# Graph attention kernel: POOL instead of DVE adds the edges' bias and makes the shared node's one-hot

## The reference, cut to what matters

```
logits  = einsum('ehd,ehd->eh', q[rows] * scale, k[cols]) + att_bias     # 8 heads of 64
row_max = segment_max(logits, rows)
p       = exp(logits - row_max[rows])
denom   = segment_sum(p, rows)
y       = segment_sum((p / denom[rows])[:, :, None] * v[cols], rows)
out     = y.reshape(n, 512) @ Wo + bo
```

## Time and profile before

| | |
|---|---|
| time, median of 3 runs | 3393.04 us (3389.54 to 3396.01) |
| the profiled execution's own time | 3388.5 us, its span 3386.7 us |
| busy over the whole span | PE 88%, DVE 85%, ACT 65%, POOL 65% |
| busy in the edge loop, 2000 to 2800 us | PE 94%, DVE 99.5%, ACT 98.4%, POOL 78% |
| the chain that ended last, by engine | POOL 26%, DVE 25%, issue 20%, PE 14%, DMA 8%, ACT 3% |

### The profile page before, as it was taken

One profiled execution on the slowest core, in us unless ns is written; L12 is line 12 of the kernel. 1 busy time (PEld: TensorE's weight loads), 2 busy tenths in 40 slices (PEclk: granted clock), 3 DMA queues, 4 the chain that ended last, 5 costly groups with the idle time before them and its releaser, 6 DMA issues.

```text
span 3386.7 us, 50546 instructions
## 1 busy us (share of the span) xinstructions
PE 2965.5 (88%) x11485; PEld 1732.4 (51%) x11610; DVE 2891.4 (85%) x8827; ACT 2207.6 (65%) x7734; POOL 2206.9 (65%) x2509
## 2 busy tenths in 40 slices
PE   6898888888887369999999999999999999889998
PEld 4554544544554135555555555555555555445554
DVE  9897777777776379999999999999999999867776
ACT  6332222222221059999999999999999999934443
POOL 0377777777777557777777777777777777511110
PEclk9898888888898689999999999999999999999999
DMA  6343333333332688878888887888888888411121
GB/s 205 81 135 102 106 107 100 102 101 107 104 104 67 224 287 256 253 253 254 256 257 254 257 259 252 258 258 253 257 256 252 257 256 259 145 66 69 68 70 55
DMA packets 258890, 615.16 MB, mean 182 GB/s; under 512 B 69451, under 2 KB 80023, under 8 KB 258338
## 3 DMA queue, kind: packets, MB, share of 16 engines
q0 software_dynamic: 144832, 443.72, 41.5%
q1 hardware_dynamic: 107414, 155.39, 15.1%
q10 hardware_dynamic: 6348, 12.80, 1.1%
HBM read 550.28 MB, written 61.49 MB: 181 GB/s over the span
## 4 chain that ended last, share of the span: by engine, by line
POOL 26%; DVE 25%; issue 20%; PE 14%; DMA 8%; ACT 3%; DVEq 2%; another core or an unknown queue 1%; ACTq 0%; SPq 0%; POOLq 0%
POOL rec_scratch L617 22%; DMA big<-kv_scratch,small 8%; DVE big L1374 6%; PE banks L1920 5%; DVE small L1272 5%; DVE big L1266 5%; PE banks L1949 4%; POOL big L638 3%; ACT big L799 3%; POOL small L645 2%; DVE big L992 2%; PE banks L1963 1%; PE banks L1874 1%; PE banks L1823 1%
## 5 line engine op out<-in xcount | busy, mean ns | idle before, releaser
L799 ACT ACTIVATE big<-big,small 128x65 f32<-128x65 f32 x6656 | 1625.9, 339 | 4.8
L638 POOL DMA_INDIRECT big<-kv_scratch,small x832 | 842.8, 1013 | 405.6 <-DVE small L1272 285.7
L617 POOL DMA_INDIRECT rec_scratch<-big,small x782 | 770.0, 985 | 340.4 <-issue 237.9
L1874 PE MATMUL banks<-big,small 128*128 128x260 f32 x3328 | 898.4, 393 | 96.1 <-POOL small L645 42.7
L1823 PE MATMUL banks<-big,small 128*128 x1664 | 876.5, 609 | 30.7 <-DMA big<-q_scratch 12.0
L1874 PEld LDWEIGHTS banks<-big,small 128*128 128x128 f32 x3328 | 597.4, 190 | 534.4 <-ACT big L799 243.0
L1374 DVE SCALAR_TENSOR_TENSOR big<-big,loS,banks 128x520 f32 x832 | 611.4, 735 | 20.2 <-PE banks L1874 18.6
L1731 PE MATMUL banks<-big 128*128 128x512 f32 (+1 forms) x1176 | 609.5, 666 | 19.5 <-DVE big L982 19.5
L1266 DVE TENSOR_TENSOR big<-banks,big 128x512 f32<-128x512 f32 x832 | 558.6, 671 | 43.9 <-PE banks L1823 25.7
L645 POOL TENSOR_SCALAR small<-iotaF,small 128x128 f32<-128x128 f32 x832 | 524.3, 630 | 54.1 <-PE banks L1874 28.2
L1272 DVE TENSOR_REDUCE small<-big 128x8 f32<-128x512 f32 x832 | 548.4, 664 | 0.0
(11 more groups left out here) (257 smaller groups left out, 2742.1 us busy)
## 6 DMA issues: line engine op xcount, KB each, us to landing
rowR<-lo_rows SPq DMA_DIRECT2D x97, 256.0 KB
big<-src_rows SPq DMA_DIRECT2D x97, 256.0 KB, 3.6
big<-in_x_dram SPq DMA_DIRECT2D x96, 256.0 KB, 2.8
big<-kv_scratch,small POOLq DMA_INDIRECT x832, 5.2
rec_scratch<-big,small POOLq DMA_INDIRECT x782
kv_scratch<-big SPq DMA_DIRECT2D x48, 260.0 KB
q_scratch<-big SPq DMA_DIRECT2D x48, 256.0 KB
kv_scratch<-big SPq DMA_DIRECT2D x48, 256.0 KB
```

Of the source, the lines that this page charges most:

```text
L617: e.indirect_dma_start(recd, bass.IndirectOffsetOnAxis(ap=ridx[:, c % 4, j:j + 1], axis=0), rec[:, 8 * c + j, :], None).then_inc(s_sc[c % ...
L638: e.indirect_dma_start(KV[:, vat(t):vat(t) + YW + D], None, KVd, bass.IndirectOffsetOnAxis(ap=recB[b_ % 4][:, t % 16, 9:10].bitcast(i32), ...
L799: ins = e.activation(heads(Vr(t), h, h + 1), heads(Vr(t), h, h + 1), ACT.Copy, scale=ph[:, h:h + 1])
L1874: ins = e.matmul(YB[t % 2][:, i, :], oh[t % 4], Vr(t)[:, 260 * i:260 * i + 260], start=True, stop=True)
```

## The change

Two instructions a block leave DVE's list and enter POOL's. `lb`, the addition of the bias, goes from DVE's step 0 (behind the last `rd`) to POOL's step 4 of the same block, in front of that step's gather. `Aoh` goes from DVE's step 6 to POOL's step 14, behind that step's gather and in front of its `one_hot`, as `last_node`; it has a semaphore of its own, `s_aoh`, for which `scale1` on PE waits. `s_bd` now rises once a block instead of twice.

```diff
+            def lb(b_):
+
+                q.wait_ge(s_rd, 16 * b_ + 16)
+                e.tensor_tensor(Lr[b_ % 2], Lr[b_ % 2], recB[b_ % 4][:, :, 0:8], ALU.add).then_inc(s_lb, 1)
+
             def one_hot(t):
...
+            def last_node(b_):
+
+                q.wait_ge(s_s1, b_)
+                e.tensor_scalar(Aoh[0:8, :], iotaF[0:8, :], llb[0:8, max(b_ - 1, 0):max(b_ - 1, 0) + 1], None, ALU.is_equal).then_inc(s_aoh, 1)
 
             for s in range(T + DEL + 2):
...
+                if s % 16 == 4 and 0 < s // 16 <= NB:
+                    lb(s // 16 - 1)
                 if s < T:
                     gather(s)
...
+                if s == 24:
+                    last_node(0)
+                if 24 < s < T and s % 16 == 14:
+                    last_node(s // 16)
                 if s - DEL - 2 >= 0:
                     one_hot(s - DEL - 2)
...
-                q.wait_ge(s_bd, 2 * b_)
+                q.wait_ge(s_bd, b_)
...
-            def lb(b_):
-
-                q.wait_ge(s_rd, 16 * b_ + 16)
-                e.tensor_tensor(Lr[b_ % 2], Lr[b_ % 2], recB[b_ % 4][:, :, 0:8], ALU.add).then_inc(s_lb, 1)
...
-                e.tensor_scalar(Aoh[0:8, :], iotaF[0:8, :], llb[0:8, max(b_ - 1, 0):max(b_ - 1, 0) + 1], None, ALU.is_equal).then_inc(s_bd, 1)
...
-                if at == 0:
-                    lb(b_)
...
-                q.wait_ge(s_bd, 2 * b_ + 2)
+                q.wait_ge(s_bd, b_ + 1)
+                q.wait_ge(s_aoh, b_ + 1)
```

More of the change, by code:

```diff
@@ L306, in build @@
         s_kv = sems("s_kv", 8)
-        s_oh, s_q1, s_pr, s_rd, s_lb, s_x2 = sem("s_oh"), sem("s_q1"), sem("s_pr"), sem("s_rd"), sem("s_lb"), sem("s_x2")
+        s_oh, s_q1, s_pr, s_rd, s_lb, s_x2, s_aoh = sem("s_oh"), sem("s_q1"), sem("s_pr"), sem("s_rd"), sem("s_lb"), sem("s_x2"), sem("s_aoh")
         s_f1, s_d1, s_zm, s_zs, s_za, s_cf = sem("s_f1"), sem("s_d1"), sem("s_zm"), sem("s_zs"), sem("s_za"), sem("s_cf")
```

## The result

The changed kernel takes 3393.99 us (median of 22 runs, 3389.41 to 3400.08), the kernel before, run beside it, 3389.49 us (median of 22, 3382.68 to 3398.11). The ratio is 1.0015, with a 95% interval of 1.0008 to 1.0021: some 5 us slower, where 10 us faster was forecast. The profiled execution has a span of 3395.4 us (before 3386.7), both at a mean granted clock of 0.941.

The account below looks back on a forecast made before the run. DVE was taken to set the pace, ACT close behind. `fwd1` 0.22 us later less 0.41 for `Aoh` gave -0.19 us a block, times 51 blocks 10 us: 3383 us from a median of 3393.04, range 3374 to 3407.

Parts of the forecast that it names:

- What bounds the kernel: Edge loop: DVE sets the pace, ACT has hardly anything in hand; the change is worth tenths of a us times 51 blocks.
- Together 0.61 us a block: DVE's list: 0.20 us back from `lb` and 0.41 from `Aoh`, 31 us over 51 blocks if nothing else changed.
- POOL, step 14: Shared node's one-hot on POOL: 0.63 us plus 0.02 between instructions, 0.65 us, arriving as 0.16 us in step 0.
- the gate: POOL, step 0's gather: 0.49 us of its 2.34 is a wait that a late POOL doesn't pay, leaving 1.84.
- Rival 2: Step 0's gather: the 0.49 us is paid anyway, `fwd1` 0.71 us late, +15 us, 3408; chance 0.18.
- POOL, step 4: The bias's addition on POOL, behind step 3's one-hot, was taken to last 0.41 us.
- rival 1: POOL's addition is dear, 0.64 us (+2 us) or 0.54 by the skill's rule (3390); 3388 to 3395; chance 0.26.
- The chain: Block's end, POOL's addition to PE's transpose to DVE's `fwd1`: DVE waits 0.42 us, `fwd1` comes 0.22 us later than before.
- From `fwd1` round to the next block's gate nothing else changes but `Aoh`: Rest of the block: only `Aoh`'s 0.41 comes off, so 0.22 - 0.41 = -0.19 us a block, 10 us.
- Late gathers: Step 15's gather often lands too late, hidden in DVE's wait before `fwd1`: nothing in the sum, up to 3 us in the range.
- ACT's cap: ACT idles 0.24 us a block, capping any DVE saving at 12 us, or 21 us with the disturbed blocks.

Follow-up runs that it names:

- e2: Changed kernel with the bias's addition back on DVE, so only the shared node's one-hot is on POOL; 3383.71 us, ratio 0.9985 to the kernel before.
- e7: Changed kernel with the shared node's one-hot in POOL's step 13 instead of 14; ratio 1.0024 to the kernel before.
- e1: Kernel before with only the bias's addition moved to POOL, `Aoh` left on DVE; 3397.0 us, ratio 1.0025.
- e11: e4 with `Bd` behind the product of step 6 instead of in front of it; ratio 0.9984 to the kernel before.
- e4: Changed kernel with `fwd1`'s output and the spread's constant in PSUM instead of SBUF; 3383.87 us, ratio 0.9983 to the kernel before.
- e9: Kernel before with 13 short dummy memsets on POOL in front of step 4's gather, nothing moved; ratio 1.0024.
- e5: Kernel before with eight short dummy memsets on POOL in front of step 4's gather, nothing moved; ratio 1.0015.

## Why the prediction was wrong, point by point

1. **What bounds the kernel, and what the change is worth at most: right.** DVE sets the pace, tenths of a us times 51 blocks: the blocks of 3 to 49 differ by 0.102 us, which by 51 is 5.2 us, and the medians by 4.5.
2. **"Together 0.61 us a block": right as DVE's entries** (0.212 + 0.385 = 0.597), **wrong as a gain.** The step that failed is "`Aoh` starts at 2270.84 and `Bd` at 2271.26: 0.42 us ... I take 0.41. `Bd` stays". `Aoh` took 0.27 us when no gather was near and 0.73 when one was the earlier trace rows; I read this as the price of `Aoh`. Half of it was the price of the gather: in blocks 3 to 49 of the kernel before, `Aoh` took 0.41 us to the next start in the 40 in which it began 0.32 us behind a gather's start, and 0.20 in the 6 with another distance. With `Aoh` gone, `Bd` stands at 0.32 us behind the same gather and pays +0.188. The move is worth 0.197, not 0.41 (one trace of e2: the same 0.197, and `lb` loses 0.056 of it).
3. **POOL, step 14: price right** (0.61 measured, 0.63 taken), **and the gate right.** The gather of step 15 comes 2.40 us behind that of step 14 and that of step 0 follows 1.85 us later (1.84 was forecast; 2.34 before). Rival 2 is out, and e7 shows it again. Counted from `fwd1`, the gather of step 0 starts at -8.03 us (median) both in the changed kernel and in e1, which has no one-hot in step 14, and the stall at `fwd1` is 0.161 against 0.154: the gate took up all of the 0.65, where I let 0.16 arrive.
4. **POOL, step 4: right.** The addition takes 0.44 us (0.41 taken), rival 1's 0.64 and 0.54 are out. The Trainium skill (GPSIMD Engine Reference, Engine selection) says about twice VectorE's time; against the 0.27 us of `lb` on DVE it was 1.6 times here.
5. **The chain: too long by a quarter of a us.** "`fwd1` comes 0.22 us later than before": measured from DVE's own steps it came 0.05 us earlier (0.161 of stall for 0.212 of `lb`). Of the 0.27 between, 0.16 is the delay that didn't arrive, 0.04 the chain from the start of the addition to `fwd1` (0.86 us at the median, 0.90 taken), and 0.06 that the addition starts 0.04 us ahead of the one-hot's recorded end rather than 0.02 behind it. This error was against the change. With it set right and nothing else, I would have forecast a still larger gain.
6. **"From `fwd1` round to the next block's gate nothing else changes but `Aoh`": the step that decides, and false.** `back1` +0.114 and the spread +0.145 are 0.26 us a block, 13 us, and with `Bd` 0.45 us, 23 us. The prediction has no term for this: it puts it at nothing. I had looked at POOL for when it is busy, when its gathers land and who waits for its results, not for what its instructions do to DVE's beside them, though the earlier trace rows show the same instruction at 0.27 and 0.73.
7. **Late gathers: larger than I allowed, and elsewhere.** The row that holds them grew by 0.10 us a block (51 x 0.10 = 5 us); I had put up to 3 us in the range, nothing in the sum, and said that they hide in the stall of `fwd1`. They stand in front of other `pr`s. On one trace each the size is uncertain: 10 waits for a gather behind `ya` in 46 blocks, before 4.
8. **ACT's cap: too tight.** I took 0.24 us of slack, 33.28 us a block at best. The median block of e11 takes 33.13, at the same work on ACT. In the changed kernel the cap never mattered: ACT waits 18.5 us over 41 waits, before 17.4 over 41.

```profile
ACT small L777 <- remote: 18.5, 41, 1.6
```

9. **Range and rivals.** 3394 lies in the range, by a mechanism that none of the rivals had. The errors had both signs: to the forecast of -0.19 us a block come +0.45 for the three hits, -0.27 for the chain and +0.10 for the gathers, which makes +0.09, where +0.10 was measured. And the 3383 was counted from the median of three runs, 3393.04, which lies 3.6 us above that of 22.

The rival that was missing reads: POOL's instructions, moved by some tenths of a us, lie down on DVE's two-input instructions. Its price could have been had from the earlier trace rows, 0.2 us for each instruction hit, and its place from the one-hot of step 4 and the gather of step 5 beside `back1` and the spread. Three such hits would have been an estimated 0.6 us a block, as much as the change takes off DVE; they were 0.45.

## What to carry to other kernels

Before you move work to POOL, list DVE's instructions that read two operands from SBUF and see which POOL instructions each of them lies beside now, and which it will lie beside after the shift: here the hits cost 0.45 us a block against the 0.60 that was taken off DVE. Two operands are not the only sign: `Aoh` has one tensor as input, in SBUF, with a column of SBUF as its scalar, and it was hit as well (0.41 for 0.20). An instruction whose duration has two values is telling of its neighbour, not of itself; if you take it away, the neighbour's price goes to the next in line. A hit instruction can be freed by one operand in PSUM or by a place behind one that doesn't compete (`pr` here); neither cost DVE anything in these traces, though the whole times of the kernels with the PSUM operands gained less than their blocks.

## What the runs showed of the hardware

**Who comes first keeps the reads, for part of its time.** These are the times from `back1`'s start to the next start against the lead of the one-hot, all from the changed kernel: lead 0.11 to 0.13 us, 0.46 to 0.48 us (38 blocks); 0.17, 0.42; 0.22, 0.37; 0.26 and more, 0.33, which is the free value. Lead and delay add up to 0.26 us each time: a one-hot that is recorded with 0.62 us and goes first holds DVE off for its first 0.26. The gathers: `Bd` 0.31 to 0.33 us behind a gather's start waits 0.22 (40 blocks), `Bd` 0.23 or 0.53 behind it doesn't wait; the spread 0.43 behind waits 0.17, 0.54 behind 0.07, 0.62 behind (the kernel before) not at all. So a gather's issue, recorded with 1.02 us, holds DVE off from somewhere between 0.23 and 0.31 to between 0.53 and 0.6 us after its start. Where DVE waits, lead and wait add up here too: to 0.60 us for the spread and `lb`, on 128 partitions, and to 0.53 to 0.54 for `Bd`, `Aoh` and the first carry, on 8. But the distance doesn't decide alone: `lb` began 0.4 to 0.6 us behind a gather's start in 32 blocks of the kernel before and waited in 5, and in 33 blocks of e2 it waited in 21. What makes the difference stays open. `pr`, `ya` and `fwd1`, with an operand in PSUM, and the reduction, with one input, show no such stretching: in the kernel before, `pr` began 0.3 to 0.4 us behind a gather's start 227 times and took 0.60 us to the next start, as it does elsewhere.

The Trainium skill (SBUF — State Buffer, Who interferes with whom) says that a DVE instruction with two inputs in SBUF contends with a GpSimd instruction that reads SBUF, and that the order of issue decides who blocks. The runs agree: `back1` 0.445 with two SBUF inputs and 0.325 with one (e4). It says of the exclusive holder that it keeps the ports for the whole instruction; for these pairs the measured wait is shorter, 0.26 of 0.62 us.

**The loser can be POOL.** In e1 the one-hot lasted 0.84 us instead of 0.62, and `back1` its short 0.41, at recorded leads of 0.08 to 0.10 us; at 0.10 to 0.14 `back1` lost. In e9 the one-hot lost up to a lead of 0.12 and won from 0.13 on, and in the changed kernel it won at 0.11. So a one-hot must be recorded some 0.1 us ahead to have the reads first, and the edge is not the same in every kernel. Nor does going first always end it: at leads of 0.27 to 0.29 us `back1` was free in e5 and the one-hot lasted 1.01 to 1.11 us in 17 of 21 blocks, while at 0.25 to 0.29 in e9 it kept its 0.62 to 0.64 us. What decides within these hundredths stays open: the records don't say when either engine asks for its operands.
